# An adaLN block on one core: the second norm's bias moved to GpSimd, FFN weight copies in three banks, steps placed anew

## The reference, cut to what matters

```
mod = (silu(c) @ wmod) -> sa, ca, ga, sb, cb, gb       # per batch, 128 each; |ga|, |gb| at least 0.25
h = layernorm(x) * (1 + ca) + sa
x = x + ga * attention(h)      # 16 heads of 8; two decayed sums over all tokens, gates, a small MLP
h = layernorm(x) * (1 + cb) + sb                        # the second norm
x = x + gb * ffn(h)            # gate and up 128 -> 352, silu(gate) * up, down 352 -> 128
# every ffn product has both operands quantised and dequantised in FP4, in blocks of 16
layernorm(x) = (x - mean) / sqrt(var + 1e-5)
```

## Time and profile before

| | us |
|---|---|
| median of 3 runs (210.63 to 212.53) | 212.3 |
| the profiled execution, its own time | 211.68 |
| its span, first to last instruction | 209.9 |
| around the span | 1.8 |
| TensorE busy | 184.1 |
| VectorE busy | 174.6 |
| GpSimd busy | 152.7 |
| ScalarE busy | 144.9 |

### The profile page before, as it was taken

The page is one execution under the profiler, slowest core; times in us unless marked ns, Lnnn a source line. Parts: engine busy times, 40 slices in busy tenths (PEclk is TensorE's granted clock), DMA queues, the critical chain, the costliest instruction groups (busy, mean ns, idle before and its releaser), DMA issues.

```text
span 209.9 us, 3498 instructions
## 1 busy us (share of the span) xinstructions
PE 184.1 (88%) x948; PEld 134.0 (64%) x948; DVE 174.6 (83%) x436; ACT 144.9 (69%) x326; POOL 152.7 (73%) x187
## 2 busy tenths in 40 slices
PE   2899845999999999879669999899999896997994
PEld 1544433476788748539537777767788484694884
DVE  3997999837898999999999999899998897776840
ACT  2578999898997999969753637654836546663642
POOL 5477363968688878979996975978867968865460
PEclk9999999699999999999999999999999999999999
DMA  5980000000000000000000100000001000011011
GB/s 168 252 218 0 2 0 0 5 0 0 0 2 3 0 0 2 0 0 5 25 0 0 30 0 19 8 27 3 25 0 45 8 25 25 0 30 52 0 52 51
DMA packets 11499, 5.66 MB, mean 27 GB/s; under 512 B 1684, under 2 KB 11352, under 8 KB 11480
## 3 DMA queue, kind: packets, MB, share of 16 engines
q1 hardware_dynamic: 11168, 5.31, 9.1%
q10 hardware_dynamic: 312, 0.13, 0.2%
HBM read 3.34 MB, written 2.10 MB: 26 GB/s over the span
## 4 chain that ended last, share of the span: by engine, by line
PE 54%; ACT 15%; issue 12%; POOL 9%; DVE 6%; DMA 2%; SPq 0%; POOLq 0%; ACTq 0%; DVEq 0%
PE pa L1089 11%; PE pa L1166 6%; PE pg L1113 5%; PE pv L1168 5%; PE pa L1190 5%; PE pv L1130 4%; POOL q_o L487 3%; POOL q_r L475 3%; PE pa L1177 3%; PE pa L1139 3%; DMA wmod_sb<-in_L_wmod_dram 2%; ACT xn L680 2%; PE pv L1149 2%; ACT L526 2%; PE pa L1185 2%
## 5 line engine op out<-in xcount | busy, mean ns | idle before, releaser
L475 POOL TENSOR_TENSOR q_r<-q_x,q_rs 128x960 f32<-128x960 f32 (+2 forms) x18 | 29.6, 1645 | 14.3 <-DVE q_rs L960 14.3
L1089 PE MATMUL pa<-wcat,hT 128*128 128x496 f32 x64 | 31.5, 620 | 5.6 <-ACT sq L606 3.4
L487 POOL TENSOR_TENSOR q_o<-q_r,q_sp 128x960 f32<-128x960 f32 (+2 forms) x18 | 29.6, 1644 | 7.2 <-DVE q_r L971 6.4
L1166 PE MATMUL pa<-guT,hqT 128*128 128x352 f32 x64 | 25.3, 477 | 4.8 <-ACT hqT L697 4.7
L1190 PE MATMUL pa<-wdg,fqT 128*128 128x128 f32 x192 | 26.9, 276 | 0.0
L706 ACT ACTIVATE sgl<-pa 128x352 f32<-128x352 f32 x32 | 14.5, 461 | 15.1 <-PE pa L1166 12.8
L1168 PE MATMUL pv<-guT,hqT 128*128 128x352 f32 x64 | 24.3, 462 | 0.3 <-DVE oc L913 0.3
L438 POOL TENSOR_TENSOR vs<-kvg,cw 128x256 f32<-128x256 f32 x32 | 20.2, 658 | 5.7 <-DVE cw L864 5.7
L1190 PEld LDWEIGHTS pa<-wdg,fqT 128*128 128x128 f32 x192 | 24.0, 192 | 0.4 <-ACT fqT L714 0.2
L1089 PEld LDWEIGHTS pa<-wcat,hT 128*128 128x128 f32 x64 | 12.0, 204 | 16.6 <-ACT sq L606 6.8
L691 ACT ACTIVATE q_A<-q_r 128x960 f32<-128x960 bf16 (+2 forms) x18 | 16.0, 888 | 8.5 <-POOL q_r L475 5.3
(11 more groups left out here) (149 smaller groups left out, 446.5 us busy)
## 6 DMA issues: line engine op xcount, KB each, us to landing
out_dram<-x_all SPq DMA_DIRECT2D x16, 128.0 KB, 1.8
x_all<-in_L_attn_x_dram SPq DMA_DIRECT2D x3, 512.0 KB, 5.3
x_all<-in_L_attn_x_dram SPq DMA_DIRECT2D x2, 256.0 KB, 3.4
wmod_sb<-in_L_wmod_dram SPq DMA_DIRECT2D x1, 256.0 KB, 5.8
wraw<-in_L_ffn_w_down_dram SPq DMA_DIRECT2D x1, 176.0 KB, 3.7
wmod_sb<-in_L_wmod_dram SPq DMA_DIRECT2D x1, 128.0 KB, 4.4
wraw<-in_L_ffn_w_gate_dram SPq DMA_DIRECT2D x1, 128.0 KB, 3.4
wraw<-in_L_ffn_w_up_dram SPq DMA_DIRECT2D x1, 128.0 KB, 3.1
```

Of the source, the lines that this page charges most:

```text
L475: g.tensor_tensor(blocks(q_r[:, s % 2, c]), blocks(q_x[:, s % 2, c]), spread(q_rs[:, s % 2, n]), ALU.mult)\
L487: g.tensor_tensor(blocks(q_o[:, s % 2, c]), blocks(q_r[:, s % 2, c]), spread(q_sp[:, s % 2, n]), ALU.mult)\
L1089: te.matmul(bank_a(("PP%d" % k, i))[:, 0:NCAT], hT[:, b, 2 * j + k, :], wcat[:, :], start=True, stop=True).then_inc(S["a_full"], 1)
L1166: te.matmul(bank_a(("G%d" % k, i))[:, 0:I], lhs, guT[:, 0, :], start=True, stop=True)\
```

## The change

It has three parts.

1. The bias of the second norm: VectorE's step L1 (one instruction per pair, 16 in all) is gone. GpSimd's step O3 has, behind the power, a wait on it and two tensor_scalar instructions of 128x1 elements each (mean times rstdb times -1), one per tile of the pair. ScalarE's L1 waits for both. VectorE's bn_aggr of pair i waits for the bias of pair i-4, since GpSimd reads the means.
2. FFN weights: the nine transposes go into three bank fillings (gate: three chunks, up: three, down: three), one semaphore step each, and ScalarE makes three copies (352, 352 and 384 columns) in place of nine.
3. All four lists are placed anew. Apart from VectorE's 16 L1 the same steps stand in them, and table loads are as many as before.

```
@@ gpsimd, in O3(i), behind the power
+                pool.wait_ge(S["rstdb"], i + 1)
+                for k in range(2):
+                    g.tensor_scalar(nmrb[:, i % 2, k:k + 1], mvb[:, i % 4, k, 0:1], rstdb[:, i % 2, k:k + 1], -1.0,
+                                    ALU.mult, ALU.mult).then_inc(S["nmrb"], 1)
@@ scalar, in L1(i)
-                act.wait_ge(S["nmrb"], i + 1)
+                act.wait_ge(S["nmrb"], 2 * i + 2)
@@ vector, in O3(i), ahead of each bn_aggr
+                    if i >= 4:
+                        dve.wait_ge(S["nmrb"], 2 * i - 6)
@@ vector
-            def L1(i):
-                dve.wait_ge(S["rstdb"], i + 1)
-                if i >= 2:
-                    dve.wait_ge(S["xn2"], 2 * i - 2)
-                v.scalar_tensor_tensor(nmrb[:, i % 2, :], mvb[:, i % 4, :, 0], -1.0, rstdb[:, i % 2, :],
-                                       ALU.mult, ALU.mult).then_inc(S["nmrb"], 1)
@@ scalar, W3
-                for k in range(6):
-                    t = bank(("WT%d" % (k + 2), 0))
...
-                    a.activation(guT[:, u, ch * P:ch * P + n], t[:, 0:n], ACT.Copy).then_inc(S["a_free"], 1)
-                for ch in range(3):
-                    t = bank(("WD%d" % ch, 0))
-                    a.activation(wdT[:, ch, :], t[:, 0:P], ACT.Copy).then_inc(S["a_free"], 1)
+                for u in range(2):
+                    t = bank(("GU%d" % u, 0))
+                    a.activation(guT[:, u, :], t[:, 0:I], ACT.Copy).then_inc(S["a_free"], 1)
+                t = bank(("WD", 0))
+                a.activation(wdT[:, :, :], t[:, 0:3 * P].rearrange("p (c d) -> p c d", c=3), ACT.Copy).then_inc(S["a_free"], 1)
@@ tensor, W3
+                for u in range(2):
+                    t = bank_a(("GU%d" % u, 0))
+                    for ch in range(3):
+                        o, n = ch * P, min(P, I - ch * P)
+                        last = te.transpose(t[:, o:o + n], w_r[0:n, (3 * u + ch) * D:(3 * u + ch + 1) * D], ident[0:n, 0:n])
+                    last.then_inc(S["a_full"], 1)
+                t = bank_a(("WD", 0))
                 for ch in range(3):
                     o = DOWN0 + CH[ch]
+                    last = te.transpose(t[:, ch * P:(ch + 1) * P], w_r[:, o:o + P], ident[:, :])
+                last.then_inc(S["a_full"], 1)
```

More of the change, by code:

```diff
@@ L65 @@
-        O3:12 QR:15 O3:13 L1:12 QO:15 L1:13 O3:14 GH:2 QR:16 QR:17 QO:16 O3:15 QO:17 L1:14 L1:15 QR:18 QR:19
-        QO:18 QO:19 GH:3 QR:20 QR:21 QO:20 QO:21""",
+        P0:0 P0:1 KC:0 XN:4 XN:5 XN:6 P0:2 XN:7 GO:0 XN:8 XN:9 GO:1 GC:0 XN:10 GB:0 P0:3 V0:0 XN:11 V1:0 V2:0
+        V3:0 GF:0 XN:12 GC:1 GB:1 W2:0 XN:13 XN:14 V0:1 V1:1 V2:1 V3:1 O3:0 GC:2 GF:1 L1:0 O3:1 GB:2 QR:4 L1:1
+        XN:15 QO:4 QR:5 O3:2 O3:3 V0:2 V1:2 V2:2 L1:2 QO:5 W3:0 GF:2 V3:2 QR:6 O3:4 L1:3 GB:3 QO:6 O3:5 L1:4
+        GO:2 QR:7 GC:3 GH:0 QR:8 QO:7 O3:6 L1:5 V0:3 QO:8 L1:6 V1:3 V2:3 QR:9 V3:3 QR:10 QO:9 O3:7 L1:7 QO:10
@@ new lines @@
+        PP:12 O2:1 GE:1 GA:2 PX:13 L1:0 O2:2 PP:13 O2:3 L1:1 GG:1 PX:14 QA:4 GD:2 GS:2 QA:5 PP:14 PX:15 N4:0
+        W3:0 L1:2 PP:15 GE:2 F1:0 L1:3 O2:4 GA:3 QA:6 N4:1 O2:5 O2:6 F1:1 L1:4 N4:2 GS:3 F1:2 QA:7 GD:3 L1:5
+        GG:2 QA:8 F3:0 N4:3 O2:7 L1:6 F4:0 F1:3 GE:3 N4:4 O2:8 F1:4 F3:1 QA:9 QA:10 F4:1 F3:2 N4:5 L1:7 F1:5
+        O2:9 F3:3 N4:6 QA:11 L1:8 F4:2 F1:6 O2:10 GG:3 L1:9 F3:4 N4:7 QA:12 O2:11 L1:10 F4:3 O2:12 F1:7 N4:8
+        F1:8 L1:11 QA:13 F3:5 F4:4 F3:6 QA:14 N4:9 O2:13 F1:9 F4:5 L1:12 QA:15 N4:10 O2:14 F4:6 F3:7 F1:10 L1:13
@@ new lines @@
+        N4:11 O2:15 F1:11 QA:16 F3:8 F4:7 QA:17 F3:9 F4:8 N4:12 L1:14 F1:12 N4:13 L1:15 F3:10 F1:13 QA:18 F3:11
+        F4:9 QA:19 F4:10 F4:11 N4:14 F1:14 N4:15 F1:15 F3:12 QA:20 F3:13 F4:12 QA:21 F4:13 F3:14 F4:14 F3:15
+        F4:15""",
+    "vector": """
+        P0:0 XN:0 XN:1 MV:0 XN:2 XN:3 SB:0 P0:1 P0:2 PP:0 PP:1 PP:2 GA:0 P0:3 PP:3 W0:0 GB:0 PP:4 W1:0 GK:0 PP:5
+        PP:6 W2:0 GE:0 PP:7 GF:0 GA:1 PP:8 PP:9 GB:1 GY:0 GG:0 GK:1 PP:10 GA:2 PP:11 O1:0 O1:1 GE:1 GF:1 O3:0
+        GB:2 O1:2 GK:2 O3:1 GG:1 O1:3 GY:1 Q:4 O3:2 QT:4 Q:5 O3:3 PP:12 GE:2 PP:13 O1:4 PP:14 GF:2 O1:5 QT:5
+        PP:15 F1:0 GA:3 Q:6 GB:3 O3:4 O1:6 GK:3 QT:6 O3:5 F1:1 GY:2 Q:7 GG:2 F1:2 Q:8 QT:7 O3:6 O1:7 GE:3 QT:8
+        O1:8 O1:9 GF:3 F1:3 Q:9 F1:4 Q:10 QT:9 O3:7 O3:8 QT:10 F1:5 Q:11 O3:9 O1:10 GY:3 GG:3 QT:11 F1:6 Q:12
+        O1:11 O1:12 O3:10 QT:12 O3:11 F1:7 Q:13 F1:8 Q:14 QT:13 O3:12 O1:13 O1:14 QT:14 F1:9 Q:15 O1:15 O3:13
+        QT:15 O3:14 F1:10 Q:16 F1:11 Q:17 QT:16 O3:15 QT:17 F1:12 Q:18 F1:13 Q:19 QT:18 QT:19 F1:14 Q:20 F1:15
+        Q:21 QT:20 QT:21""",
@@ L93 @@
[L93 to L96, removed]
+        PP:6 PX:8 PX:9 GC:0 PP:7 GE:0 PP:8 PX:10 PP:9 PX:11 PP:10 V0:0 V1:0 V2:0 V3:0 PP:11 GG:0 PX:12 GC:1 O1:0
@@ new lines @@
+        O1:1 GE:1 O2:0 PP:12 O2:1 O3:0 O1:2 V0:1 PX:13 V1:1 O3:1 V2:1 O1:3 O2:2 V3:1 PP:13 O2:3 O3:2 GG:1 PX:14
+        GC:2 O3:3 GE:2 O1:4 PP:14 PX:15 O1:5 N4:0 W3:0 PP:15 F1:0 O2:4 N4:1 O3:4 V0:2 V1:2 O1:6 O2:5 O2:6 V2:2
+        O3:5 F1:1 V3:2 N4:2 F1:2 O3:6 O1:7 GC:3 GG:2 O1:8 F3:0 N4:3 GE:3 O2:7 O1:9 F4:0 F1:3 N4:4 O2:8 F1:4 O3:7
+        F3:1 V0:3 F4:1 V1:3 O3:8 V2:3 F3:2 N4:5 F1:5 O2:9 F3:3 V3:3 O3:9 N4:6 O1:10 F4:2 F1:6 O2:10 GG:3 O1:11
+        O1:12 F3:4 O3:10 N4:7 O2:11 F4:3 O3:11 O2:12 F1:7 N4:8 F1:8 F3:5 F4:4 F3:6 O3:12 O1:13 O1:14 N4:9 O2:13
@@ L97 @@
+        F1:9 F4:5 O1:15 N4:10 O2:14 O3:13 F4:6 F3:7 O3:14 F1:10 N4:11 O2:15 F1:11 O3:15 F3:8 F4:7 F3:9 F4:8
+        N4:12 F1:12 N4:13 F3:10 F1:13 F3:11 F4:9 F4:10 F4:11 N4:14 F1:14 N4:15 F1:15 F3:12 F3:13 F4:12 F4:13
         F3:14 F4:14 F3:15 F4:15""",
@@ L250, in adaln_block_kernel @@
         fills_a = {"CT": ["CT"], "WK": ["WT1"], "CM": ["CM"], "WQ": ["WT0"], "KW": ["KW"], "MB": ["MB%d" % b for b in range(NB)],
-                   "W3": ["WT%d" % k for k in range(2, 8)] + ["WD0", "WD1", "WD2"],
+                   "W3": ["GU0", "GU1", "WD"],
                    "PX": ["XT"], "PP": ["PP0", "PP1"], "GG": ["WM"], "O2": ["OT"], "N4": ["HQT"], "F1": ["G0", "G1"],
@@ L1065, in W3 @@
                 pe.wait_ge(S["w_hq"], 1)
[L1066 to L1069, removed]
+                for u in range(2):
[5 more added lines that the diff above has]
+                t = bank_a(("WD", 0))
                 for ch in range(3):
                     o = DOWN0 + CH[ch]
-                    te.transpose(bank_a(("WD%d" % ch, 0))[:, 0:P], w_r[:, o:o + P], ident[:, :])\
-                        .then_inc(S["a_full"], 1)
+                    last = te.transpose(t[:, ch * P:(ch + 1) * P], w_r[:, o:o + P], ident[:, :])
+                last.then_inc(S["a_full"], 1)
             def PX(i):
```

38 lines of the change are left out of this document (7 added, 31 removed).

## The result

The changed kernel took 215.83 us (median of 4 runs, 214.79 to 216.55), the kernel before 212.42 us beside it. The ratio is 1.017, interval 1.012 to 1.021: slower, by 3.4 us. The forecast was 209.8 us with a range up to 212.9. It had the wrong sign.

A forecast was written before the change was run, and what follows sets the result against it. Bounds: TensorE to about 70 us, VectorE's list (GpSimd close behind) to about 165, then the last pairs' chain. Sum: 211.7 with -1.0 - 1.5 - 0.4 + 0.8 + 0.2 = -1.9 gives 209.8 us, range 206.8 to 212.9.

The forecast's parts named there:

- Part 1b: GpSimd's two new bias instructions, 0.25 us each, 0.54 us a pair with the wait; +0.8 us gets through to the end.
- the stall at 106 us: VectorE's bias lasting 1.59 us from 106.31 beside GpSimd's line 487; without it the next step starts 1.5 us sooner.
- The cover: GpSimd's idle time before its next instruction that waits for VectorE, said to hide all but 0.8 us of the new work.
- where TensorE holds: Stage to about 70 us where the first four pairs fall; nothing charged there, 0.6 us if that cover is gone.
- the list of idle times: Eleven GpSimd idle times for pairs 4 to 15, from 88.66 to 176.64 us, 0.17 to 2.03 us, counted as cover.
- Part 1a: VectorE's 16 bias instructions go: -2.5 us, 1.0 from 14 unhindered ones and 1.5 from one stalled; between 1.0 and 4.5.
- Rival A: VectorE's instructions come sooner but wait for TensorE, so only the long stall counts: -0.5 us, 211.2 us; chance 0.27.
- stay as they are: The last 30 us, the chain of the last pairs, were to run as before, lists nearly unchanged from Q:18 on.
- Part 2: Three FFN weight copies for nine on ScalarE, 1.4 us rather than 2.0: -0.4 us, range 0 to 1.0.
- Part 3: The newly placed lists: +0.2 us, from GH:3 going ahead of QO:16; other moves nothing, range -2 to +2.
- L1:14 behind N4:12: On ScalarE, this move was to give back 0.8 us after GH:3 made QO:16 and N4:12 0.6 us late.

The follow-up runs named there:

- pool_dummy: Kernel before, VectorE's bias kept, plus on GpSimd after each of the 16 powers a wait and two unread 128x1 instructions: 215.16 us, ratio 1.012.
- part1: Kernel before with only the bias moved to GpSimd, VectorE's 16 L1 taken out, other lists as before: 216.79 us, ratio 1.022.
- fill_after: Changed kernel with 12 unread identity transposes on TensorE just ahead of its wait for q_o of step 16: 213.77 us, ratio 1.009.
- fill_part1_free_bank: Kernel before with the bias on GpSimd, plus 9 identity transposes into a free bank ahead of TensorE's q_o transposes of step 16: 214.83 us, ratio 1.013.
- no_bias_new_lists: Changed kernel (three-bank copies, new orders) with the second norm's bias left out altogether: 212.81 us, ratio 1.000.
- the second dose of load: Kernel before, VectorE's bias kept, with four unread 128x1 GpSimd instructions a pair rather than two: 219.48 us, ratio 1.035.
- part2: Kernel before with only three bank fillings and three copies for the FFN weights: 213.31 us, ratio 1.004.

## Why the prediction was wrong, step by step

The changed kernel's end stands at +4.1 us in the table. Its parts: part 1 +3.0, part 2 -0.6, the lists +0.6 to step 16; then +1.1 for the half clock near the end. From there to the span: the point at 51 us came 0.6 us sooner in it (50.87 for 51.51), and 209.9 + 4.1 - 0.6 = 213.4.

- **Part 1b, the step that failed most (+0.8 forecast, about +2.2 by pool_dummy).** The size was right: 0.28 us an instruction, 8.5 us in all, GpSimd at 161.0. The cover was wrong. It took GpSimd's idle time before its next wait for VectorE, and never asked who waits for what GpSimd does in between. Of the first four pairs, "where TensorE holds", nothing was charged; but V3:1 stands behind two of these powers, TensorE, VectorE and the first quantiser step wait for it in turn, and 1.3 us are lost by step 4. Of the pairs 7 to 14, 0.11 + 0.37 = 0.5 us was charged; 2.1 came, where a q_r or q_o with little or no idle time ahead of it follows the power (0.6 of it at 144 us, shown above). By luck not all of the loss is left in the total: the lateness took 1.2 us off the stall at 106 us. Also, the 1.28 us in the list of idle times lie ahead of line 462 at 161.33 and aren't a wait for VectorE.
- **Part 1a (-2.5 forecast, -1.0 measured without load).** The stall at 106 us was priced at its full 1.5 us; moving the bias away from it gave 0.3, since half a microsecond of it came back as a new stall and as much as a wait for TensorE. And relief and load don't add: -1.0 + 2.2 = 1.2, but part1 has 3.0 at step 16. Of the 1.8 between them 0.8 is the stall of line 955 at 96.79 us, and 0.7 the stall at 106 us, which the load alone had nearly undone, so that the relief couldn't win it again. The other 0.3 isn't traced. Rival A (VectorE waits for TensorE instead) described this, but it was priced with a load that was too small.
- **The clock was in no term and in no rival.** The last 30 us were to "stay as they are". They cost 1.1 us more, with a half-clock stretch in them. The other variants without added transposes have one there too, costing 1.1 to 1.6 us, except the kernel before and the two with unread load. Where transposes filled the gap without pushing what follows, taking it away was worth 1.1 us (fill_after) and 1.6 us (fill_part1_free_bank) by the table.
- **Part 2 (-0.4 forecast, -0.6 measured)** was right.
- **Part 3 (+0.2 forecast, +0.6 measured at step 16, +0.2 at the end)** was right in size and wrong inside. With GH:3 back the lists are level with the old ones at step 16 (+2.3 and +2.4) and 0.4 us ahead at the end (+3.5 and +3.9). GH:3 made QO:16 0.6 us late, as worked out, and QO:17 only 0.2, but the end keeps 0.6: what L1:14 behind N4:12 was to give back doesn't show. Of the other moves, the gain of 2.7 us at step 4 was in no term, nor was its loss. One place that loses, VectorE and GpSimd in the changed kernel:

```profile
79.70 2.02 DVE L841 TENSOR_TENSOR zb<-kvg,bias 128x384 f32<-128x384 f32 x1
```

```profile
79.50 0.62 POOL L426 TENSOR_TENSOR mrt<-mask,rt 128x256 f32<-128x256 f32 x1
80.09 1.21 POOL L438 TENSOR_TENSOR vs<-kvg,cw 128x256 f32<-128x256 f32 x2
```

A product of two inputs that took 0.82 us for this batch in the kernel before (at 80.2) stands here behind two GpSimd instructions. TensorE then idles 2.38 us ahead of line 1137, and has half clock in what follows:

```profile
85.74 0.66 PE L1137 MATMUL pa<-ident,oc 128*128 128x128 f32 x4 [2.38 <-DVE oc L914]
...
88.12 1.38 PE L1164 MATMUL pa<-guT,hqT 128*128 128x352 f32 x2
```

No run here mends this place alone, so its share isn't measured. It isn't what takes the early gain back: in no_bias_new_lists the same product takes 0.71 us and the clock stays whole at 87 us, and yet the gain is gone by step 6. What does is open.

Put together in the forecast's own sum: 209.8 + 1.4 (1b) + 1.5 (1a) + 1.8 (what the two don't add up to) - 0.2 + 0.4 (parts 2 and 3) + 1.1 (clock) - 0.6 (ahead of 51 us) = 215.2 us, and the profiled execution took 215.16. The sum closes because the 1.8 is what was missing between part1 and its two halves; it tests nothing more.

## What to carry to other kernels

Before work goes to an engine with idle time, list for each instruction behind it who waits for its result and how long that engine could be late, from that engine's side; idle time in the loaded engine's own list is only half of the answer, and here the second dose of load cost more than the first. Load an engine with work that nobody reads to measure that slack before writing the real thing. And where two versions differ by a per cent, read the granted clock of each run first: a gap filled with spare transposes into a bank that is already free was worth 1.6 us in part1, more than part 2 or the new lists.

## What the runs showed that was not expected

- Half clock followed idle times of TensorE of 1.83 us ahead of 177.30 in the changed kernel, 1.29 us ahead of 174.22 in part2 and 1.24 us in part1; but it didn't follow 1.27 us ahead of 175.41 in the kernel before, which kept 2.4 GHz. What sets the two apart isn't settled by these rows; runs of one kernel differ too.
- A transpose of the identity lasts some 0.13 us (9 in 1.15 us), and with 9 of them in the gap the clock stayed whole; but it has to wait for the bank that it writes: into the bank that ScalarE was still emptying, the end lies at +4.3 us, into a free one at +3.0.
- A stall between VectorE and GpSimd doesn't vanish with the instruction that had it. With the bias gone from VectorE a stall stands on line 955 in part1 and on line 841 in the changed kernel; with the bias moved it has one of 0.66 us itself.
